# Heads in pairs on the row halves of the scores, and the next graph's products spread between this graph's stages

## The chip, the core and the metric

The program runs on one NeuronCore of a Trainium2 chip. The number that counts is the device time of one launch, in microseconds (us), lower being better. Five things work side by side: TensorE (PE, matmuls, with PEld for its weight loads), VectorE (DVE), ScalarE (ACT), GpSimd (POOL), and SyncE (SP), which only issues DMAs. They meet through semaphores. Every engine carries out its own instructions in the order in which they are written.

## What is computed

Sixteen graphs of 512 nodes with 384 features go through two attention layers, each with a layer norm, a ReLU and a residual. The first has 6 heads of 64 features with a softmax over masked scores; the second has 12 heads of 32 features, whose scores come from a sum of one source and one destination value, a leaky ReLU and a masked softmax, then an ELU and a gate.

```python
h = relu(layernorm(x))
q, k, v = heads(h @ Wq + bq), heads(h @ Wk + bk), heads(h @ Wv + bv)
probs = softmax(q @ k.T / sqrt(64) + where(adj, 0, -9e15))          # 6 heads
x = x + (probs @ v) @ Wf + bf
h = relu(layernorm(x))
f = h @ W                                                          # 12 heads of 32
a = leaky_relu(tanh(f) @ w_src + (tanh(f) @ w_dst).T)
o = elu(softmax(where(adj, a, -999)) @ f + b)
g = sigmoid(h @ H_w.T + H_b)
x = x + g * o + (1 - g) * h
```

## The kernel before

Everything of a graph stays on the chip. 512 nodes are four tiles (TT) of 128 partitions, 384 features three chunks (FC). A product in `fp32r` is made of three terms, high times high, high times low and low times high, so every operand has a `_hi` and a `_lo` tensor; `three` issues the nine matmuls of such a product. ACT makes the high part out of PSUM (`turned_high`, `qk_hi`, `ctx_high`), DVE the low part (`turned_low`, `qk_low`, `ctx_low`).

The order is written out by hand: each engine has a function `graph(b, more)` that is one turn of a loop over the graphs, and semaphores tie the five orders together. In one turn PE does, in this order:

- **first attention**: `turn_probs(b, h, c)` transposes a chunk of a head's probabilities into a `turn` bank (line 1094), DVE (even c) or ACT (odd c) copies it to `pT`, and `context` multiplies it with `v_tok` (line 1113). Between the turns of head h stand the `scores` of head h + 2 (lines 1083 and 1084), the products for q and k of the third pair of heads, and the transposes of half the mask.
- **projection and second norm**: `by_node(b, "out", ...)`, residual, statistics, `turn_norm`, one gate product.
- **features and logits**: `by_feature(..., "w1", c)`, `logits`; then DVE, ACT and PE in turns make the rows from which the second layer's weights come (`uq`, `r_rows`), beside `turn_feat` and the gate products.
- **aggregation**: `spread` puts four heads' rows into four banks (line 1154); in 12 steps DVE makes three edge tiles (line 818), ACT and POOL the fourth (lines 581, 584 and 412), and `aggregate` adds eight matmuls on quarters of the array's columns (lines 1170 and 1174). After the steps 0 to 7 PE also does the next graph's `turn_norm`, four of its q and k products and a `values` product; before step 11 stand its first two scores.
- **tail**: `turn_sums` (line 1187) with the next graph's scores and the rest of `values` between; DVE's `divide`, `positive`, `difference`, ACT's `elu` and POOL's `add_out` finish this graph, and SP stores it.

A score tile is one head by 128 queries by 512 keys. The head's 64 features fill only half the rows, so q's high and low part lie under each other in `qs`, k's high part is there twice in `kh` (POOL copies it, `double_keys`), and `kl` holds k's low part with zeros below: two full 128-row matmuls give three terms. DVE adds the mask and takes the minimum (`maxima`, line 771) into the two-deep ring `sm`, ACT takes the exponential (`exps`, line 533), DVE the reciprocal of the sum (`inverse`, line 776, once per head), POOL multiplies (`normalise`, line 356).

Eight PSUM banks: two `work`, two `score`, two `turn`, two `acc`. The work banks are handed out in alternation by the place of a product in the list TURN. The turned input `hT_hi`/`hT_lo` exists once, so the next graph's `norm1` may only be turned in after this graph's last gate product.

```python
q = qs[:, s, i, t * P:(t + 1) * P]
nc.tensor.matmul(score[n % 2][:], q, kh[:, s, i], start=True, stop=False)
nc.tensor.matmul(score[n % 2][:], q, kl[:, s, i], start=False, stop=True).then_inc(score_full, 1)
```

## Time and profile before

| what | value |
|---|---|
| device time, three runs | 2077.71, 2081.09, 2085.63 us, median 2081.09 |
| the profiled execution's span, first to last instruction | 2077.5 us |
| PE busy | 1859.4 us, 90% |
| DVE busy | 1414.8 us, 68% |
| ACT busy | 1201.8 us, 58% |
| POOL busy | 1098.2 us, 53% |
| DMA | 46.29 MB, mean 22 GB/s |

No separate time outside the span is given for the profiled execution; the median is 3.6 us above its span. PE's busy time counts a matmul from its start to its modelled end, and neighbours overlap by some 0.16 us, so the pace of a stream of matmuls is read from start to start in the timeline.

### The profile page before, as it was taken

The numbers are of one execution on the slowest core, as the hardware profiler recorded it, in microseconds if no ns is written. First come the engines' busy times: TensorE is split into PE (matmuls) and PEld (weight loads), VectorE is DVE, ScalarE is ACT, GpSimd is POOL, SyncE is SP. The second block draws the span as 40 slices with busy tenths as digits, with TensorE's granted clock in tenths as the row PEclk, the third lists the DMA queues.
The fourth block names the chain that finished last, engine by engine and source line by source line (L and its number), as shares of the span: only waits on it lengthen the run. The fifth ranks groups of instructions, "written<-read, shape, count | busy, mean of one in ns | idle before, by whom it ended". The sixth has DMA issues, their size and how long they took to land.

```text
span 2077.5 us, 35937 instructions
## 1 busy us (share of the span) xinstructions
PE 1859.4 (90%) x10608; PEld 1117.5 (54%) x10608; DVE 1414.8 (68%) x3115; ACT 1201.8 (58%) x2311; POOL 1098.2 (53%) x1383
## 2 busy tenths in 40 slices
PE   5998898988999989899999999889898899999986
PEld 4555555555554555546556465555555555455552
DVE  5667576675757667586775857757667575766757
ACT  4566465664656656565564656646566465665654
POOL 3455555464554655445554555555546455465545
PEclk9999999999999999999999999999999999999999
DMA  4001001010000101001010010100101000010000
GB/s 135 1 1 51 0 11 39 0 50 0 20 31 0 50 0 50 0 0 50 0 50 0 4 47 0 50 0 11 39 0 50 0 21 30 0 50 0 31 1 16
DMA packets 38101, 46.29 MB, mean 22 GB/s; under 512 B 2624, under 2 KB 38080, under 8 KB 38080
## 3 DMA queue, kind: packets, MB, share of 16 engines
q1 hardware_dynamic: 38080, 46.03, 6.7%
q8 instruction: 11, 0.18, 0.0%
q14 instruction: 10, 0.08, 0.0%
HBM read 33.44 MB, written 12.58 MB: 22 GB/s over the span
## 4 chain that ended last, share of the span: by engine, by line
PE 42%; issue 21%; POOL 19%; DVE 9%; ACT 7%; DVEq 0%; POOLq 0%; ACTq 0%
PE work L1022 16%; PE acc L1170 7%; PE acc L1174 6%; POOL arena L356 6%; POOL fin_g L421 4%; ACT arena L533 3%; POOL xres L435 3%; PE turn L1094 3%; PE acc L1133 2%; PE score L1083 2%; POOL xres L423 2%; POOL arena L403 2%; POOL arena L412 2%; DVE arena L818 2%; PE score L1084 2%
## 5 line engine op out<-in xcount | busy, mean ns | idle before, releaser
L533 ACT ACTIVATE arena<-sm,nmax 128x512 f32<-128x512 f32 x384 | 275.9, 719 | 142.3 <-DVE nmax L771 140.7
L412 POOL TENSOR_TENSOR arena<-arena,adjT 128x512 f32<-128x512 f32 x192 | 224.0, 1167 | 249.2 <-ACT arena L584 242.4
L356 POOL TENSOR_SCALAR arena<-arena,rinv 128x512 f32<-128x512 f32 x384 | 281.7, 753 | 126.6 <-DVE rinv L776 126.6
L771 DVE CUSTOM_DVE_ANT_0 sm<-score,mask 128x512 f32<-128x512 f32 x384 | 255.0, 680 | 66.3 <-PE score L1084 50.9
L818 DVE SCALAR_TENSOR_TENSOR arena<-score,uqT,adjT 128x512 f32<-128x512 f32 x384 | 269.8, 744 | 16.7 <-PE acc L1174 11.4
L1094 PEld LDWEIGHTS turn<-ident_f,arena 128*128 128x128 f32 x1536 | 180.6, 140 | 137.5 <-issue 78.3
L1094 PE MATMUL turn<-ident_f,arena 128*128 128x128 f32 x1536 | 242.8, 278 | 12.6 <-POOL arena L356 7.7
L1170 PE MATMUL acc<-arena 128*32 128x512 f32 x1536 | 204.5, 604 | 38.7 <-POOL arena L412 28.0
L786 DVE COPY arena<-turn 128x512 f32<-128x512 f32 x192 | 132.4, 689 | 129.2 <-PE turn L1094 128.4
L1083 PE MATMUL score<-kh,qs 128*128 128x512 f32 x384 | 183.6, 478 | 39.3 <-DVE nmax L771 39.2
L1174 PE MATMUL acc<-arena,u_den 128*32 128x512 f32 x1536 | 200.2, 592 | 0.0
L1113 PE MATMUL acc<-arena,v_tok 128*64 128x512 f32 x768 | 193.0, 609 | 5.6 <-DVE arena L786 5.6
L545 ACT ACTIVATE arena<-turn 128x512 f32<-128x512 f32 x192 | 112.8, 587 | 129.9 <-PE turn L1094 127.8
L364 POOL TENSOR_TENSOR rstd<-var,mhalf 128x1 f32<-128x1 f32 x128 | 68.3, 551 | 216.4 <-DVE var L730 216.4
L581 ACT ACTIVATE arena<-turn,nqT 128x512 f32<-128x512 f32 x192 | 131.1, 683 | 66.8 <-PE turn L1154 63.5
L1084 PE MATMUL score<-kl,qs 128*128 128x512 f32 x384 | 151.9, 396 | 0.0
L584 ACT ACTIVATE arena<-arena,uqT 128x512 f32<-128x512 f32 x192 | 138.8, 723 | 6.3
L818 DVE SCALAR_TENSOR_TENSOR arena<-turn,uqT,adjT 128x512 f32<-128x512 f32 x192 | 142.4, 742 | 0.0
L403 POOL TENSOR_TENSOR arena<-arena,uqT 128x384 f32<-128x384 f32 x64 | 60.3, 942 | 147.3 <-DVE uqT L936 147.3
L421 POOL TENSOR_TENSOR fin_g<-arena 128x384 f32<-128x384 f32 x64 | 73.2, 1144 | 120.2 <-DVE arena L848 115.5
L743 DVE SCALAR_TENSOR_TENSOR hT_lo<-work,hT_hi 128x384 fp32r<-128x384 f32 x128 | 70.8, 554 | 81.6 <-ACT hT_hi L501 81.4
L496 ACT ACTIVATE hn<-xres,shift,rstd 128x384 f32<-128x384 f32 x64 | 45.3, 707 | 137.9 <-DVE shift L735 137.9
(138 smaller groups left out, 4100.5 us busy)
## 6 DMA issues: line engine op xcount, KB each, us to landing
x_in<-in_x SPq DMA_DIRECT2D x16, 768.0 KB, 5.8
xres<-in_x SPq DMA_DIRECT2D x16, 768.0 KB, 4.6
out_x<-xres SPq DMA_DIRECT2D x64, 192.0 KB, 1.9
adj_u<-in_adj SPq DMA_DIRECT2D x16, 256.0 KB, 6.0
arena<-in_wq SPq DMA_DIRECT2D x1, 576.0 KB, 6.3
arena<-in_wk SPq DMA_DIRECT2D x1, 576.0 KB, 7.4
arena<-in_wv SPq DMA_DIRECT2D x1, 576.0 KB, 8.5
arena<-in_wf SPq DMA_DIRECT2D x1, 576.0 KB, 9.6
```

The lines of the kernel that those rows point to most:

```text
L356: nc.gpsimd.tensor_scalar(pr, pr, rinv[:, h, t:t + 1], 1.0, ALU.mult, ALU.mult).then_inc(probs_ready, 1)
L412: nc.gpsimd.tensor_tensor(edge[:, (n * HG + HG - 1) % 8], t_ring[:, n % 2], adjT[:, n % TT], ALU.mult).then_inc(last_edge_ready, 1)
L533: nc.scalar.activation(probs[h % 3][:, t], sm[:, i % 2], ACT.Exp, scale=-1.0, bias=nmax[:, h, t:t + 1], accum_out=rsum[:, h, t:t + 1]).the ...
L771: nc.vector.tensor_tensor_reduce(sm[:, i % 2], score[i % 2][:], mask[:, t], 1.0, 3.0e38, ALU.add, ALU.min, nmax[:, h, t:t + 1]).then_inc(s ...
L818: nc.vector.scalar_tensor_tensor(out=edge[:, (n * HG + j) % 8], in0=rbank[j][:], scalar=uqT[:, c, q:q + 1], in1=adjT[:, c], op0=ALU.max, o ...
L1022: ins = nc.tensor.matmul(ps, l(c), r(c), start=(c == 0 and i == 0), stop=(c == FC - 1 and i == 2))
L1083: nc.tensor.matmul(score[n % 2][:], q, kh[:, s, i], start=True, stop=False)
L1084: nc.tensor.matmul(score[n % 2][:], q, kl[:, s, i], start=False, stop=True).then_inc(score_full, 1)
L1094: ins = nc.tensor.transpose(turn[c % 2][:, t * P:(t + 1) * P], probs[h % 3][:, t, c * P:(c + 1) * P], ident_f[:])
L1113: ins = nc.tensor.matmul(acc[p % 2][i * DH0:(i + 1) * DH0], v_tok[:, c, f:f + DH0], (pT_late if p == 2 else pT_early)[i][:, c], start=(c = ...
L1170: nc.tensor.matmul(acc[0][j * DH1:(j + 1) * DH1], h_tok[:, c, f:f + DH1], edge[:, (n * HG + j) % 8], start=(c == 0), stop=(c == TT - 1), s ...
L1174: ins = nc.tensor.matmul(acc[1][j * DH1:(j + 1) * DH1], u_den[:, c, g, j], edge[:, (n * HG + j) % 8], start=(n == 0), stop=(n == STEPS - 1 ...
```

## The change

**Scores.** `qs`, `kh` and `kl` go. `qk_hi` and `qk_lo` hold q and k of all three pairs, head 2p in rows 0 to 63 and head 2p + 1 in rows 64 to 127. A step of `scores(g, p, t)` makes the tiles of both heads: three terms by two heads, six matmuls of 64 rows, alternating between the row halves, each half into its own bank. `double_keys` and the zeros go; the copies of a product out of PSUM (`qk_hi_copy`, `qk_low`) are one instruction of 128 rows where there were two of 64. `ctx_hi` and `ctx_lo` lie where q was.

**Order.** The six shared banks (two `work`, four `score`) are given out by a table, HOME, with two semaphores each; `turn` banks are now the work banks. Attention goes by pairs p: for each chunk c both heads are turned, then come score tiles of pair p + 1, then the context of chunk c - 1; `inverse` and `normalise` go tile by tile. `sm` is four deep. There are two turned-input buffers, `hT[0]` for the first norm and `hT[1]` for the second, so the next graph's norm1, its statistics and its q, k products move out of the aggregation: norm1's statistics stand between pairs 0 and 1 on DVE (and `root`, `norm1` on POOL), its turns in pair 2, k0 behind attention, k1 and k2 in the second norm, q0 before `uq`, q1 before the last gate product, q2 at the end. `gate` product 0 now stands before `logits(2)`, all four adjacency turns behind `out`.

```diff
-            def scores(g, h, tiles=range(TT)):
-                s, i = (h // 2) % 2, h % 2
...
-                    q = qs[:, s, i, t * P:(t + 1) * P]
-                    nc.tensor.matmul(score[n % 2][:], q, kh[:, s, i], start=True, stop=False)
-                    nc.tensor.matmul(score[n % 2][:], q, kl[:, s, i], start=False, stop=True).then_inc(score_full, 1)
+            def scores(g, p, t):
...
+                for i in range(2):
+                    bank_free(pe, g, "s", p, t, i)
+                q = slice(t * P, (t + 1) * P)
+                terms = ((qk_hi, qk_hi), (qk_lo, qk_hi), (qk_hi, qk_lo))
+                for n, (l, r) in enumerate(terms):
+                    for i in range(2):
+                        rows = slice(i * DH0, (i + 1) * DH0)
+                        ins = nc.tensor.matmul(bank_of(g, "s", p, t, i)[:], l[rows, 0, p, q], r[rows, 1, p],
+                                               start=(n == 0), stop=(n == len(terms) - 1))
...
+HOME = {
+    ("k", 0): 0, ("k", 1): 5, ("k", 2): 2, ("q", 0): 1, ("q", 1): 1, ("q", 2): 0,
...
+    ("fin", 0): 1, ("fin", 1): 0, ("fin", 2): 0, ("fin", 3): 0,
+}
...
+S_TILES = ((0, 1), (2,), (3,), ())
...
             def graph(b, more):
+                for p in range(NPAIR):
+                    for c in range(TT):
+                        turn_probs(b, p, c)
+                        if p + 1 < NPAIR:
+                            for t in S_TILES[c]:
+                                scores(b, p + 1, t)
+                        elif more:
+                            turn_norm(b + 1, 0, c)
+                        if c > 0:
+                            context(b, p, c - 1)
+                    context(b, p, TT - 1)
```

PE in the aggregation:

```diff
                 for n in range(STEPS):
                     if more and n == STEPS - 1:
-                        scores(b + 1, 0, (0, 1))
+                        scores(b + 1, 0, 0)
                     aggregate(b, n)
...
-                    if n == 3:
-                        hT_ready(b + 1, "norm1")
-                    if n in (3, 4, 5, 6):
-                        query_key(b + 1, (n - 3) // 2, "kq"[n % 2])
-                    if n == 7:
-                        values(b + 1, 0)
```

DVE: the statistics behind the first pair, and the tail:

```diff
+                    if p == 0 and more:
+                        dve.wait_ge(x_loaded, 16 * b + 32)
+                        for step in (tile_stats, mean, variance, shifts):
+                            for t in range(TT):
+                                step(b + 1, 0, t)
...
+                for t in range(TT):
+                    inverse_den(b, t)
+                    if more and t < 2:
+                        maxima(b + 1, 0, t + 2)
+                    divide(b, t)
+                    if more:
+                        inverse(b + 1, 0, t)
+                    if t > 0:
+                        difference(b, t - 1)
+                    positive(b, t)
+                difference(b, TT - 1)
+                if more:
+                    qk_low(b + 1, 2, "q")
```

POOL in the tail:

```diff
-                add_out(b, 0)
-                if more:
-                    normalise(b + 1, 0)
-                add_out(b, 1)
-                add_out(b, 2)
-                add_out(b, 3)
+                for t in range(TT):
+                    if more:
+                        normalise(b + 1, 0, t)
+                    if t > 0:
+                        add_out(b, t - 1)
+                add_out(b, TT - 1)
```

PE, in attention: a turn is line 1094 before and 989 now (`arena` is where the probabilities lie), scores are lines 1083 and 1084 before and 978 now, context is line 1113 before and 1005 now. Before, one head:

```order
L1094 MATMUL turn<-ident_f,arena 128x128 x4
L1083 MATMUL score<-kh,qs 128x512
L1084 MATMUL score<-kl,qs 128x512
L1094 MATMUL turn<-ident_f,arena 128x128 x4
L1083 MATMUL score<-kh,qs 128x512
L1084 MATMUL score<-kl,qs 128x512
```

Now, a pair:

```order
L989 MATMUL work<-ident_f,arena 128x128 x8
L978 MATMUL score<-qk_hi 128x512 x2
L978 MATMUL score<-qk_hi,qk_lo 128x512 x2
L978 MATMUL score<-qk_lo,qk_hi 128x512 x2
L1005 MATMUL acc<-arena,v_tok 64x512 x2
L989 MATMUL work<-ident_f,arena 128x128 x8
```

Four score matmuls for a pair of tiles became six on half the rows, and every step now passes from whole-array turns to row halves to column halves and back.

DVE, between the first and the second pair: 667 to 681 are the statistics of the next graph's norm1 (672, 676 and 681 the last of them), 722 is the copy of a turned chunk, 712 `maxima`; REGISTER_ALU and ISA rows without operands prepare a wait. Now:

```order
L670 REGISTER_ALU
L672 BN_AGGR mv<-stats 128x2
L676 TENSOR_SCALAR var<-mv 128x1 x4
L681 SCALAR_TENSOR_TENSOR shift<-mv,rstd 128x1 x4
L722 COPY arena<-work 128x512
L275 REGISTER_ALU
L708 REGISTER_ALU
L712 ISA sm,nmax<-score,mask 128x512
```

Before, in the same place, between the second and the third head's turns:

```order
L771 ISA sm,nmax<-score,mask 128x512
L771 ISA nmax 128x1
L757 SCALAR_TENSOR_TENSOR kl<-work,bias_c,kh 64x512 x2
L776 RECIPROCAL rinv<-rsum 128x4
L791 SCALAR_TENSOR_TENSOR ctx_lo<-acc,bias_c,ctx_hi 128x512
L786 COPY arena<-turn 128x512
```

The statistics, whose last four instructions wait for POOL's `root`, came from behind the second norm to ahead of a copy for which PE's turn bank waits.

DVE, in the tail: 825 (759 now) reads a turned sum, 831 (764) is `divide`, which frees its work bank, 848 (777) `difference`, 842 (772) `positive`. Before:

```order
L825 RECIPROCAL rden<-work 128x12
L765 REGISTER_ALU
L771 ISA sm,nmax<-score,mask 128x512
L771 ISA nmax 128x1
L830 REGISTER_ALU
L831 TENSOR_TENSOR arena<-work,rden 128x384
L848 SCALAR_TENSOR_TENSOR arena<-arena 128x384
```

Now:

```order
L759 RECIPROCAL rden<-work 128x12
L708 REGISTER_ALU
L712 ISA sm,nmax<-score,mask 128x512
L712 ISA nmax 128x1
L708 REGISTER_ALU
L712 ISA sm,nmax<-score,mask 128x512
L712 ISA nmax 128x1
L764 TENSOR_TENSOR arena<-work,rden 128x384
L718 RECIPROCAL rinv<-rsum 128x2
L777 SCALAR_TENSOR_TENSOR arena<-arena 128x384
```

Two score tiles now stand between reading a turned sum and dividing it, and the divide frees the bank in which PE's next `values` product or turn is due.

## Rows read from the trace of the kernel before

**Rows 1.** First lines of the page: the span, and busy time by engine.

```profile
span 2077.5 us, 35937 instructions
...
PE 1859.4 (90%) x10608; PEld 1117.5 (54%) x10608; DVE 1414.8 (68%) x3115; ACT 1201.8 (58%) x2311; POOL 1098.2 (53%) x1383
```

**Rows 2.** Stretches: length, busy of PE, PEld, DVE, ACT, POOL, clock, DMA.

```profile
1013.36:1056.29 42.93, 40.72 (x276) 18.67 (x275) 34.63 (x54) 26.70 (x43) 23.43 (x28) 1.00 0.00 0
1056.29:1069.48 13.19, 10.66 (x59) 8.40 (x56) 11.27 (x28) 8.38 (x20) 8.31 (x8) 1.00 0.04 15
1069.48:1108.76 39.28, 36.67 (x203) 22.02 (x201) 24.09 (x57) 24.67 (x55) 23.00 (x31) 1.00 0.18 62
1108.76:1124.19 15.43, 12.91 (x67) 10.78 (x66) 10.23 (x28) 5.89 (x11) 7.09 (x11) 0.89 0.00 0
1124.19:1133.50 9.31, 9.30 (x33) 5.45 (x33) 2.50 (x15) 4.50 (x8) 5.59 (x10) 1.00 0.00 0
1133.50:1139.95 6.45, 5.72 (x34) 4.62 (x34) 4.98 (x13) 4.57 (x9) 0.80 (x1) 1.00 0.00 0
2027.90:2060.90 33.00, 27.39 (x214) 9.17 (x213) 25.63 (x38) 18.06 (x28) 18.42 (x20) 1.00 0.01 1
```

**Rows 3.** Timeline of PE in the last graph's aggregation: start, us, instruction, wait.

```profile
2027.90 0.62 PE L1154 MATMUL score<-r_rows,pick 128*128 128x512 f32 x2
...
2038.49 0.72 PE L1154 MATMUL score<-r_rows,pick 128*128 128x512 f32 x2
...
2042.50 1.07 PE L1170 MATMUL acc<-arena 128*32 128x512 f32 x8 [0.97 <-POOL arena L412]
...
2048.49 0.73 PE L1154 MATMUL score<-r_rows,pick 128*128 128x512 f32 x2
```

**Rows 4.** Timeline of PE in attention: turns, scores and context.

```profile
1087.37 0.61 PE L1094 MATMUL turn<-ident_f,arena 128*128 128x128 f32 x4
...
1088.29 0.60 PE L1094 MATMUL turn<-ident_f,arena 128*128 128x128 f32 x4
...
1097.48 0.66 PE L1094 MATMUL turn<-ident_f,arena 128*128 128x128 f32 x4
1098.07 1.08 PE L1113 MATMUL acc<-arena,v_tok 128*64 128x512 f32 x4
1099.08 0.66 PE L1094 MATMUL turn<-ident_f,arena 128*128 128x128 f32 x4
```

**Rows 5.** Timeline of PE: first and last of a product's nine matmuls, and the next.

```profile
1080.43 0.40 PE L1022 MATMUL work<-hT_hi,wk_hi 128*128 128x512 f32 x1
...
1082.54 0.40 PE L1123 MATMUL work<-ident_b,mask 128*128 128x128 bf16 x4
```

**Rows 6.** Groups of weight loads: busy us, mean ns, idle before.

```profile
L1094 PEld LDWEIGHTS turn<-ident_f,arena 128*128 128x128 f32 x1536 | 180.6, 140 | 137.5 <-issue 78.3 <-POOL arena L356 16.3 <-DVE arena L786 10.8
L1084 PEld LDWEIGHTS score<-kl,qs 128*128 128x128 f32 x384 | 73.4, 191 | 0.7
```

**Rows 7.** Timeline of DVE: norm1's statistics, from first to last.

```profile
997.05 1.93 DVE L721 BATCH_NORM_STATS2 stats<-x_in 128x6 f32<-128x384 f32 x4
...
1001.56 0.16 DVE L735 SCALAR_TENSOR_TENSOR shift<-mv,rstd 128x1 f32<-128x1 f32 x1 [0.36 <-POOL rstd L364]
```

**Rows 8.** Groups of the page: the chain from a turned chunk to probabilities.

```profile
L533 ACT ACTIVATE arena<-sm,nmax 128x512 f32<-128x512 f32 x384 | 275.9, 719 | 142.3 <-DVE nmax L771 140.7
...
L356 POOL TENSOR_SCALAR arena<-arena,rinv 128x512 f32<-128x512 f32 x384 | 281.7, 753 | 126.6 <-DVE rinv L776 126.6
L771 DVE CUSTOM_DVE_ANT_0 sm<-score,mask 128x512 f32<-128x512 f32 x384 | 255.0, 680 | 66.3 <-PE score L1084 50.9
...
L786 DVE COPY arena<-turn 128x512 f32<-128x512 f32 x192 | 132.4, 689 | 129.2 <-PE turn L1094 128.4
```

**Rows 9.** Timeline of POOL in the tail: two starts of `add_out`.

```profile
1070.00 1.01 POOL L421 TENSOR_TENSOR fin_g<-arena 128x384 f32<-128x384 f32 x1
...
1072.24 1.01 POOL L421 TENSOR_TENSOR fin_g<-arena 128x384 f32<-128x384 f32 x1
```

More of the change, by code:

```diff
@@ L63 @@
[L63 to L80 removed]
+NSM = 4
@@ new lines, with both, attention_order @@
+for _t in range(TT):
+    HOME["norm1", _t] = 2 + _t
+    for _p in range(NPAIR):
+        for _i in range(2):
+            HOME["turn", _p, _t, _i] = _i
+            HOME["s", _p, _t, _i] = 2 + 2 * (_t % 2) + _i
+S_TILES = ((0, 1), (2,), (3,), ())
+def both(name, p, t):
+    return [(name, p, t, 0), (name, p, t, 1)]
+def attention_order():
+    order = []
+    for p in range(NPAIR):
+        for c in range(TT):
+            order += both("turn", p, c)
+            if p + 1 < NPAIR:
+                for t in S_TILES[c]:
+                    order += both("s", p + 1, t)
+            else:
+                order += [("norm1", c)]
+    return order
@@ new lines, with of_next @@
+FIRST = ([("norm1", t) for t in range(TT)]
+         + [("k", 0), ("q", 0), ("k", 1), ("k", 2), ("q", 1), ("q", 2), ("v", 0), ("v", 1), ("v", 2), ("v", 3)]
+         + [x for t in range(TT) for x in both("s", 0, t)])
+TURN = attention_order() + MIDDLE + TAIL
+def of_next(name):
+    return name[0] in ("norm1", "k", "q", "v") or name[:2] == ("s", 0)
+LAST = [x for x in TURN if not of_next(x)]
+def place(g, *name):
+    bank = HOME[name]
+    first, turn, last = ([x for x in order if HOME[x] == bank] for order in (FIRST, TURN, LAST))
+    if of_next(name):
+        if isinstance(g, int) and g == 0:
+            return bank, first.index(name)
+        return bank, len(first) + (g - 1) * len(turn) + turn.index(name)
+    own = last if isinstance(g, int) and g == B - 1 else turn
+    return bank, len(first) + g * len(turn) + own.index(name)
@@ L474, in _ @@
             make_mask(0)
-            double_keys(0, 0, (mask_ready, 1))
-            double_keys(0, 1)
-            normalise(0, 0)
+            for t in range(TT):
+                normalise(0, 0, t)
             with pool.Fori(0, B - 1) as b:
@@ L760, in qk_low @@
-                mark_drained(ins, g, name, p)
-            def maxima(g, h, tiles=range(TT)):
-                for t in tiles:
-                    i = h * TT + t
-                    dve.wait_ge(score_full, g * NH0 * TT + i + 1)
-                    if i >= 2:
-                        dve.wait_ge(exp_ready, g * NH0 * TT + i - 1)
-                    settle(dve)
-                    nc.vector.tensor_tensor_reduce(sm[:, i % 2], score[i % 2][:], mask[:, t], 1.0, 3.0e38,
-                                                   ALU.add, ALU.min, nmax[:, h, t:t + 1]).then_inc(smax_ready, 1)
@@ L929, in graph @@
                 gate_sum(b, 1)
+                if more:
+                    qk_low(b + 1, 0, "q")
                 filled(dve, b, "uq", 0)
@@ new lines, in graph @@
+                    context(b, p, TT - 1)
+                if more:
+                    hT_ready(b + 1, 0)
+                    query_key(b + 1, 0, "k")
+                pe.wait_ge(split, len(names))
+                pe.wait_ge(ctx_ready, (b + 1) * NPAIR)
+                for t in range(TT):
+                    by_node(b, "out", ctx_hi, ctx_lo, "wf", t)
+                for c in range(TT):
+                    turn_adj(b, c)
+                turn_norm(b, 1, 0)
+                turn_norm(b, 1, 1)
@@ L1309, in _ @@
                 values(0, t)
-            scores(0, 0)
-            scores(0, 1)
+            for t in range(TT):
+                scores(0, 0, t)
             pe.wait_ge(consts_ready, 1)
```

840 lines of the change are left out of this document (375 added, 465 removed).

## The prediction, made before the changed kernel was run

> **What bounds the kernel now.** I read the page's first lines, then the stretches of one graph in the middle, then PE's timeline inside each, then what each gap waits for. PE is busy 90% of a span of 2077.5 us, the next engine, DVE, 68% [rows 1]. The stretches cut one turn of 126.6 us at PE's landmarks [rows 2]: aggregation 42.9 (first spread to last aggregate), tail 13.2, attention 39.3, projection with the second norm 15.4, features and logits 9.3, and 6.45 to the next spread. PE is busy 40.7 of the 42.9, 36.7 of the 39.3, 9.3 of the 9.3, but 10.7 of 13.2 in the tail and 12.9 of 15.4 in the second norm, where the clock also falls (mean 0.89). So PE's order bounds it nearly everywhere, with some 10 us of gaps a graph. A change pays only by fewer PE columns, or by putting PE work into those gaps without opening others.
>
> How large can others be? The last graph shows it: its aggregation has none of the next graph's work, and takes 33.0 us with PE busy for 27.4 [rows 2]. There DVE's edges, and the ACT and POOL chain for the fourth edge tile, set the pace: the spreads are 10.6 and 10.0 us apart, and the aggregate waits 0.97 us for POOL [rows 3]. So 12 us of PE work stood in this stage before and cost 9.9. Taken out, it gives back 9.9 and must find room elsewhere.
>
> **Scores.** A turn of four transposes with one head's score tile takes 0.92 us [rows 4], and nine 512-column matmuls 2.11, 0.234 each [rows 5]. A pair of tiles was four such matmuls, 0.94 us. Now it is three terms of two. If the row halves run side by side as the column quarters do (eight aggregate records in 1.07 us, where the same number, at context's pace of four records in 1.01 by pairs, would take some 3.7 alone [rows 3, 4]), the pair costs 3 x 0.234 = 0.70; if one after the other, 1.40. No row shows two row halves at once, so these are both ends. I take 0.70, since column halves, the nearest form, overlap: two halves by two records make 1.01 us in context [rows 4]. The weights needn't stand in the way: a term needs two loads of 128 columns, which last 191 ns each, but loads of 140 ns follow each other every 0.11 us in the turns, so they overlap [rows 4, 6]. Changing the shape costs: a turn behind context takes 0.59 where behind scores it takes some 0.40 [rows 4]. I put 0.1 us on each side of a score step (between 0 and 0.2). So 0.9 against 0.94, twelve times a graph: nearly nothing, -0.5 us. POOL's doubling and the second halves of the copies go; in attention these engines were not the bound.
>
> The Trainium skill speaks here too. TensorEngine Tiling (Array Packing), section Tiling Modes, says that changing the tiling mode drains TensorE, which the trace agrees with for columns. TensorE: Matmul & The Clock Gate, Part 3, gives 3.07x for four row tiles, not 4x; an estimate from that page is 0.30 us a term instead of 0.234, 2.5 us a graph, and the sum would come to some 2120. No row here shows row tiles.
>
> **Aggregation, from 42.9 to 35.4.** Base is the last graph's 33.0. Added: q1 (2.1 us) ahead of gate 3, so DVE's gate_sum and qk_low come between edges(0) and edges(1), and edges(1) starts 2 us later; POOL's chain is late there too, so I count 0.65. The mask (four POOL operations, 2.75 us, between the fourth edges of steps 4 and 5) was covered by PE's products; now POOL is on the path: +1.4. The pair of scores before step 11 and its switches: +0.4 net of the gap there. Sum 35.4; bounds 33.9 (nothing but the scores) and 38.
>
> **Tail, from 13.2 to 18.5.** PE's work is now three pairs of scores, four values products of 1.6, four turns of sums of 0.4, and q2: 12.7 us. It hands banks back and forth with DVE. values(1) needs the bank of fin 0, whose divide stands behind two maxima of the score step between: gap 1.5. fin 2 needs fin 1 divided, behind the next two maxima (0.68 each [rows 8]), which only start when the scores after values(1) are full: gap 2.0. q2 ends at 16.8 and its bank is the first that the next attention turns into; ACT's and DVE's copies take until 18.4. POOL is as late: four normalise pairs of 1.35 with two add_outs of 2.24 between [rows 9] end near 18.6. Bounds: 14 (POOL and DVE keep up) and 21.
>
> **Attention, from 39.3 to 39.1 with k0.** For pairs 0 and 1 PE's steps sum to 11.1 us (32 turns 3.5, four score steps 3.6, four contexts 4.0). Behind the last turn stands a chain: copy 0.69, two maxima 0.68 each, two exponentials 0.72, inverse, normalise 0.75 [rows 8], about 5 us with hand-overs, beside two contexts of 1.0. So the next pair starts 12.4 us after this one, 1.3 of it idle. In pair 1 DVE first has the statistics, 4.7 us from first to last [rows 7], of which the four BN_STATS are 1.93 and the end waits for POOL's roots. Before they stood in the features stage, where DVE was idle (2.5 busy of 9.3 [rows 2]) and cost nothing. Now the copy of the first chunk is queued behind them, PE's second turn waits for its bank, and I get 2.4 us of gap and 15.0 for the pair. Pair 2 with norm1's turns: 9.5; k0: 2.2, which hides ctx 2's copies. Bounds: 36 (the chain is hidden), 42.
>
> **Second norm, from 15.4 to 13.8; features, from 9.3 to 11.3; to the spread, from 6.45 to 8.3.** Projection 6.4, adjacency 1.0, turns and k1, k2 fill what was idle, with 0.6 us of gaps: 13.8, now with 4.2 us of products in it. Gate 0 moved into the features: +1.7 with its switch. Before the spread stand q0 and its copies: qk_low is queued ahead of uqT on DVE, so `rlo` comes 1.9 us later.
>
> **The sum.** 35.4 + 18.5 + 39.1 + 13.8 + 11.3 + 8.3 = 126.4 against 126.6: -0.2 a turn, -3 us in fifteen. The first graph has two more products ahead of attention (+2), the last graph has no statistics and no fills (-5). My walk is at full clock; the stretch of before has one at mean 0.89, 15.4 x 0.11 = 1.7 us slower at most. Such falls follow weak PE stretches, and the new tail is one, so I add 0.5 us a graph: +7.5. Span 2077.5 - 3 - 3 + 7.5 = 2079; the median of the runs lies 3.6 above the span, so **2082 us**. Each graph's bound is off by perhaps 2 us either way, 30 in all: that is the true width.
>
> **Rivals.**
> (a) The row halves don't overlap fully, a slower outcome. Fully serial costs 0.70 x 12 = 8.4 us a graph, 126 in all: 2208. Half-way, with two weight loads of 0.19 as the pace (0.38 a term [rows 6]), 5 us a graph: 2158. The change pays nothing from 0.25 us a term on. For it: no row shows it done; against: the column tiles.
> (b) The new waits are smaller than I walk them, faster: the aggregation comes to 34, the tail to 16.5, pair 1 to 14: -4.4 a graph, 2016. For it: by my walk PE stands idle for about 6 us in the tail and 5 in attention, where before it was idle for 2.5 and 2.6 [rows 2], so hand-overs that overlap better than I count give much back.
> (c) The waits are larger: POOL is later in the tail (its two add_outs and four normalise pairs have no slack there), and the second norm's chain slips behind ACT's adjacency copies: +3 us a graph, 2127.
> (d) The products moved don't leave a mark at all and everything is as before: 2082, the same as the forecast.
>
> **Chances.** Forecast and (d), within 2065 to 2100: 0.32 (of it 0.05 faster, 0.21 same, 0.06 slower). (a) 0.2, (b) 0.33, (c) 0.15. A measurement of this kernel tells about 0.5% from no change, 10 us. Faster by more: 0.05 + 0.32 = 0.37; same: 0.21 + 0.02 = 0.23; slower: 0.40. The range for 8 in 10 takes in (b) to 2015 and (a) to its middle: 2015 to 2145.
>
> **What the new profile would show.** Score groups: six matmuls of 64 rows in about 0.7 us from first to last start, both halves starting within some 10 ns; (a) if they start 0.2 apart. The spreads 11 us apart, and the whole aggregation near 35. In attention a wait of PE for DVE's copy behind the statistics, 2 to 3 us once a graph, and POOL as releaser of the first turn of each pair. In the tail two gaps of 1.5 to 2 us behind DVE's divide. PE busy nearer to 85% than to 90%. If a graph takes 122 us, my waits in tail and attention were too long; if 130 or more, look at the score steps first.

## The result, and the profile of the changed kernel

The changed kernel takes 2182.34 us (median of four runs, 2181.36 to 2185.67), the kernel before 2082.4 in the same comparison: a ratio of 1.0496, 95% interval 1.0477 to 1.0516. The forecast was 2082, the range 2015 to 2145. The change makes the kernel 5% slower, and the prediction missed that.

The first lines of the page of after answer to [rows 1]; `PEclk` is from its view in 40 slices.

```profile
span 2183.5 us, 35601 instructions
...
PE 1870.5 (86%) x10992; PEld 1116.4 (51%) x10992; DVE 1369.7 (63%) x3114; ACT 1115.0 (51%) x2215; POOL 1039.1 (48%) x1287
...
PEclk9999999999999999999999999998999989989998
```

PE is busy 11 us more than before in a span 106 us longer, every other engine less. The time went into waits of PE, and part of PE's busy time is the lower clock: its mean is 0.963, where before it was 0.989.

One turn, for a graph in the middle (aggregation, tail, attention with k0, second norm, features, to the next spread). The columns are those of [rows 2]. Two landmarks lie 0.5 us earlier than there: the aggregation ends here with the start of its last matmul, the features with the start of the last logits product.

```profile
1061.06:1096.41 35.35, 30.00 (x228) 11.01 (x228) 27.31 (x42) 19.10 (x30) 21.14 (x24) 1.00 0.02 7
1096.41:1116.81 20.40, 14.73 (x87) 10.98 (x80) 14.98 (x36) 10.67 (x26) 10.00 (x10) 1.00 0.03 10
1116.81:1160.43 43.62, 39.13 (x213) 22.03 (x214) 26.01 (x75) 22.34 (x51) 24.75 (x35) 0.92 0.13 42
1160.43:1174.55 14.12, 13.13 (x83) 11.56 (x82) 10.19 (x26) 7.46 (x14) 7.25 (x11) 1.00 0.06 22
1174.55:1185.37 10.82, 10.82 (x42) 6.82 (x41) 1.10 (x2) 4.22 (x7) 0.77 (x2) 1.00 0.00 0
1185.37:1194.14 8.77, 7.89 (x45) 6.32 (x44) 5.94 (x16) 5.57 (x11) 0.68 (x1) 1.00 0.00 0
```

Graphs differ, so the comparison needs the mean of each stage over the first fourteen turns, cut at these landmarks, before and after. "Walked" is the prediction's own figure. By the landmark of [rows 2], to which the walked 35.4 and 18.5 belong, the two entries 35.35 and 20.4 of the last column are 35.9 and 19.9:

| stage | before | walked | after | after, at full clock |
|---|---|---|---|---|
| aggregation | 42.4 | 35.4 | 36.4 | 35.35 |
| tail | 13.7 | 18.5 | 21.1 | 20.4 |
| attention, k0 | 39.3 | 39.1 | 42.7 | 41.55 |
| second norm | 15.3 | 13.8 | 13.75 | 13.75 |
| features, to the spread | 16.3 | 19.6 | 19.6 | 19.6 |
| sum | 127.0 | 126.4 | 133.6 | 130.7 |

The last column is the length in graphs where the granted clock stayed at 2.4 GHz in that stage (the second norm varies between 13.4 and 14.1 at full clock, so its mean stands). Attention has three such graphs: 41.56 and 41.54 us where the tail before it was at full clock too, and 40.94 where the tail had a mean clock of 0.92; the first two stand in the table. Two rows to compare with the stretches above, an aggregation with a mean clock of 0.95 and an attention with 1.00:

```profile
926.44:963.40 36.96, 31.62 (x227) 11.41 (x228) 27.30 (x42) 19.08 (x30) 21.13 (x24) 0.95 0.02 7
...
322.55:364.11 41.56, 36.38 (x214) 20.62 (x214) 25.81 (x75) 22.02 (x51) 24.76 (x35) 1.00 0.14 44
```

So an aggregation takes 36.96 or 35.35 us, an attention 43.62 or 41.56, and the difference goes with the clock. Over the whole span the trace of after has 41 stretches at 1.2 GHz, 164 us together; before has 12, 50 us.

Which waits of PE there are, the view of waits shows, first of before and then of after (us in total, times, longest):

```profile
PE score L1083 <- DVE nmax L771: 39.2, 64, 0.9
PE acc L1170 <- POOL arena L412: 28.0, 34, 1.0
PE work L1037 <- ACT hn L496: 26.0, 45, 1.1
```

```profile
PE acc L1060 <- POOL arena L408: 68.0, 64, 2.1
PE work L989 <- POOL arena L374: 50.1, 76, 1.8
PE work L1076 <- DVE arena L764: 34.4, 17, 2.1
PE work L989 <- DVE qk_lo L697: 26.7, 14, 2.5
PE work L921 <- DVE arena L764: 22.9, 15, 1.5
PE work L989 <- DVE arena L722: 21.0, 15, 1.8
```

Before, the three longest sums were waits of at most 1.1 us, and after the first graph's start none was over 1.3. Now aggregates wait for POOL's fourth edge (line 408), the turns (line 989) for POOL's `normalise` (374), DVE's copy of q2 (697) and its copy of a chunk (722), and the tail's products and turns for DVE's `divide` (764). Each is over 20 us in all.

### The profile page after: what moved, and what is told of

Its sections match the earlier page's. It is cut to its first block, busy times and chain, and to the rows that moved or that the text cites. A ratio compares the mean times of both kernels' runs of the same rounds, so it can differ in the third digit from the quotient of the medians.

```text
span 2183.5 us, 35601 instructions
## 1 busy us (share of the span) xinstructions
PE 1870.5 (86%) x10992; PEld 1116.4 (51%) x10992; DVE 1369.7 (63%) x3114; ACT 1115.0 (51%) x2215; POOL 1039.1 (48%) x1287
## 4 chain that ended last, share of the span: by engine, by line
PE 49%; issue 20%; POOL 14%; DVE 10%; ACT 7%; POOLq 1%; DVEq 1%; ACTq 0%; DMA 0%
PE score L921 10%; PE work L921 8%; PE work L989 7%; PE score L978 6%; PE acc L1005 5%; POOL arena L408 4%; PE acc L1060 4%; PE acc L1064 4%; POOL arena L374 3%; DVE sm L712 3%; ACT arena L511 2%; PE acc L1024 2%; POOL arena L401 2%; POOL mask L366 1%; PE score L936 1%
## 5 line engine op out<-in xcount | busy, mean ns | idle before, releaser
L753 DVE SCALAR_TENSOR_TENSOR arena<-score,uqT,adjT 128x512 f32<-128x512 f32 x576 | 395.4, 744 | 104.8 <-PE acc L1064 93.1
L989 PE MATMUL work<-ident_f,arena 128*128 128x128 f32 x1536 | 248.3, 295 | 98.4 <-POOL arena L374 50.1
L989 PEld LDWEIGHTS work<-ident_f,arena 128*128 128x128 f32 x1536 | 178.2, 146 | 254.5 <-issue 127.9
L548 ACT ACTIVATE arena<-score,nqT 128x512 f32<-128x512 f32 x192 | 130.5, 680 | 213.8 <-PE score L1045 188.8
L517 ACT ACTIVATE arena<-work 128x512 f32<-128x512 f32 x192 | 114.0, 594 | 196.5 <-PE work L989 193.9
L722 DVE COPY arena<-work 128x512 f32<-128x512 f32 x192 | 132.0, 687 | 106.7 <-PE work L989 106.2
L1064 PEld LDWEIGHTS acc<-arena,u_den 128*32 128x32 f32 x1536 | 53.7, 113 | 119.7 <-issue 119.7
L978 PE MATMUL score<-qk_hi 64*128 64x512 f32 x384 | 98.8, 504 | 12.0 <-DVE nmax L712 11.0
L697 DVE SCALAR_TENSOR_TENSOR qk_lo<-work,bias_c,qk_hi 128x512 fp32r<-128x512 f32 x64 | 47.9, 749 | 86.3 <-ACT qk_hi L494 86.3
L921 PE MATMUL work<-wv_hi,hT_hi 128*128 128x384 f32 x192 | 75.1, 391 | 27.3 <-DVE arena L764 22.9
```

Of the source, the lines that this page charges most:

```text
L753: nc.vector.scalar_tensor_tensor(out=edge[:, (n * HG + j) % 8], in0=score[j][:], scalar=uqT[:, c, q:q + 1], in1=adjT[:, c], op0=ALU.max, o ...
L921: ins = nc.tensor.matmul(ps, l(c), r(c), start=(c == 0 and i == 0), stop=(c == FC - 1 and i == 2))
L978: ins = nc.tensor.matmul(bank_of(g, "s", p, t, i)[:], l[rows, 0, p, q], r[rows, 1, p], start=(n == 0), stop=(n == len(terms) - 1))
L989: ins = nc.tensor.transpose(bank_of(b, "turn", p, c, i)[:, t * P:(t + 1) * P], probs[p % 2 * 2 + i][:, t, c * P:(c + 1) * P], ident_f[:])
L1064: ins = nc.tensor.matmul(acc[1][j * DH1:(j + 1) * DH1], u_den[:, c, g, j], edge[:, (n * HG + j) % 8], start=(n == 0), stop=(n == STEPS - 1 ...
```

## Experiments

**First question: waits, clock or row halves?** In PE's timeline of attention in after, two score records (both halves of a term) start together, a term 0.23 us after the last, and a score step takes 0.90 us from its start to that of the context:

```profile
1122.50 0.50 PE L978 MATMUL score<-qk_hi 64*128 64x512 f32 x2
1122.84 0.39 PE L978 MATMUL score<-qk_hi,qk_lo 64*128 64x512 f32 x2
1123.07 0.40 PE L978 MATMUL score<-qk_lo,qk_hi 64*128 64x512 f32 x2
1123.40 1.08 PE L1005 MATMUL acc<-arena,v_tok 128*64 128x512 f32 x4
```

That was the forecast's number, so the row halves were no suspect. My theory was one part lower clock, one part waits in the tail and at pair 1. The next kernels took these one by one.

**e1_warm** fills PE's known waits with 34 products a graph that nobody reads.

```diff
+            def warm(k, n):
+                for _ in range(n):
+                    nc.tensor.matmul(acc[k][:, 0:D], w_hi["wk"][:, 0, 0:P], w_hi["wk"][:, 0, :], start=True, stop=True)
...
                 if more:
+                    warm(0, 6)
                     values(b + 1, 1)
                     scores(b + 1, 0, 3)
+                    warm(0, 8)
```

> The changed kernel with idle-filling matmuls on TensorE: 34 extra matmuls of 384 columns a graph (0.177 us each, 6 us a graph) into an accumulator bank that is overwritten afterwards, put just ahead of the waits of the tail, of the pair boundaries and of the copy behind the statistics. Theory C (the half clock, which the new waits bring on, costs about half of the 105 us lost): the time at half clock falls from 164 us to under 70 us and the kernel gets 20 to 50 us faster in spite of the added work, 2130 to 2165 us. Theory W (the waits alone are the cost, the half clock falls in places that wait anyway): unchanged or slower by up to 6 us a graph, 2180 to 2270 us.

2155.33 us, ratio 1.0334 (1.0314 to 1.0355), clock 0.987, time at 1.2 GHz 58 us in place of 164. PE is busy 53 us more, and the kernel is some 30 us faster. So the lower clock does cost time: about a third of the loss went with it, by the ratios. Every tail and every attention between the first graph and the last is at full clock in e1, and they take 20.4 and 41.56 us, as in after at full clock, so the fills lie inside the waits and lengthen no stage. What is left at 1.2 GHz stands mostly in the aggregation, behind the wait that follows the mask. The rest of the loss is waits and longer steps.

**e2_divide_first** puts `divide` ahead of the two maxima in the tail.

```diff
                     inverse_den(b, t)
+                    divide(b, t)
                     if more and t < 2:
                         maxima(b + 1, 0, t + 2)
-                    divide(b, t)
```

> The changed kernel with one swap on VectorE in the tail: divide stands ahead of the two maxima instead of behind them. Theory W: the gaps of 1.5 and 2.1 us before values(1) and the third turned sum shrink by 1.3 us each, the tail of 20.4 us gets 1 to 2.5 us shorter, 2145 to 2170 us. Rival P (GpSimd's chain of normalise and add_out ends the tail, the gaps on TensorE are slack): the gaps go and the time stays, 2178 to 2190 us.

2140.34 us, ratio 1.0263 (1.0241 to 1.0284), a little more than expected. The tail goes from 20.4 to 17.9 us in its median.

**e3_late_shifts** takes norm1's four `shifts`, which wait for POOL's roots, out from in front of pair 1's first copy.

```diff
                         elif more:
                             turned_low(b + 1, 0, c)
+                        if p == 1 and c == 0 and more:
+                            for t in range(TT):
+                                shifts(b + 1, 0, t)
...
-                        for step in (tile_stats, mean, variance, shifts):
+                        for step in (tile_stats, mean, variance):
```

> The changed kernel with the four shift instructions of norm1's statistics, which wait for GpSimd, moved behind the first copy and the first maxima of the second pair. Theory W: the wait of TensorE's second turn falls from 1.4 us by about 1.4 us, and with it 1 to 3 us a graph, 2135 to 2168 us. Theory C adds that a clock fall goes with it in some graphs. If the boundary chain hides it: 2178 to 2190 us.

2140.04 us, ratio 1.0266 (1.0246 to 1.0287); attention 42.7 to 40.55 in the mean. The wait it removes is seen in after, on DVE and then on PE:

```profile
1133.98 0.16 DVE L681 SCALAR_TENSOR_TENSOR shift<-mv,rstd 128x1 f32<-128x1 f32 x1 [0.48 <-POOL rstd L381]
...
1135.54 0.18 DVE L681 SCALAR_TENSOR_TENSOR shift<-mv,rstd 128x1 f32<-128x1 f32 x1 [0.36 <-POOL rstd L381]
1135.64 0.68 DVE L722 COPY arena<-work 128x512 f32<-128x512 f32 x1
```

```profile
1136.37 1.09 PE L989 MATMUL work<-ident_f,arena 128*128 128x128 f32 x8 [1.38 <-DVE arena L722]
```

**e4_halves_in_turn** writes head 0's three terms and then head 1's three, to price the overlap.

```diff
-                for n, (l, r) in enumerate(terms):
-                    for i in range(2):
+                for i in range(2):
+                    for n, (l, r) in enumerate(terms):
```

> The changed kernel with the six score matmuls of a pair of tiles in another order: all three terms of the first head, then all three of the second, so that the row halves can't run side by side for two of three terms. If side by side is worth 0.234 us a term, this costs 0.47 to 0.7 us per pair of tiles, twelve a graph: 60 to 130 us more, 2240 to 2315 us. If the score steps are hidden behind other waits: under 40 us more. If the halves gain nothing by alternating: unchanged.

2185.55 us, ratio 1.0503 (1.0469 to 1.0537): no change, so the expectation of 60 to 130 us more fell. The records say why: the first terms of both heads start 10 ns apart though two other matmuls stand between them in the order as written, and the step is as long as before:

```profile
431.17 0.51 PE L978 MATMUL score<-qk_hi 64*128 64x512 f32 x2
431.51 0.40 PE L978 MATMUL score<-qk_hi,qk_lo 64*128 64x512 f32 x2
431.74 0.40 PE L978 MATMUL score<-qk_lo,qk_hi 64*128 64x512 f32 x2
432.07 0.64 PE L1060 MATMUL acc<-arena 128*32 128x512 f32 x4
```

**e11_halves_serial** forces the order with a wait.

```diff
-                for n, (l, r) in enumerate(terms):
-                    for i in range(2):
+                for i in range(2):
+                    if i == 1:
+                        filled(pe, g, "s", p, t, 0)
+                    for n, (l, r) in enumerate(terms):
```

> The changed kernel with the six score matmuls of a step in the order head 0's three terms, head 1's three, and a wait of PE between for the first three to be done. It asks what the overlap of the row halves is worth. A score pair then takes 1.4 us plus one wait of PE for its own semaphore (0.1 to 0.3) in place of 0.70. If PE is the bound at all score steps: 12 x 0.9 = 11 us a graph, 160 us more than the changed kernel, 2345. If PE's time at the score steps in the tail and at the pair boundaries lies beside other engines' work: half of that or less, 2230 to 2260. If the halves did not overlap in the first place, nothing changes but the wait, 12 x 0.2 = 2.4 us a graph, 2220.

2429.93 us, ratio 1.170 (1.166 to 1.174). In its timeline one head's three terms take as long as both heads' did, then comes the wait, then the other head:

```profile
1244.63 0.50 PE L980 MATMUL score<-qk_hi 64*128 64x512 f32 x1
1244.97 0.39 PE L980 MATMUL score<-qk_hi,qk_lo 64*128 64x512 f32 x1
1245.21 0.39 PE L980 MATMUL score<-qk_lo,qk_hi 64*128 64x512 f32 x1
1245.65 0.49 PE L980 MATMUL score<-qk_hi 64*128 64x512 f32 x1
```

A step is 1.02 us to the other head's first term, and some 0.9 more for that head, 1.9 in place of 0.90: 1.0 more, 12 us a graph, if all of it counted. At full clock the stages show 7.5 of these: aggregation 36.35 for 35.35, tail 22.2 for 20.4, attention 45.6 for the 40.94 that stands, like it, behind a tail below full clock. The measured loss is 248 us, more than I expected in any case: 447 us of this span are at 1.2 GHz (clock 0.908), 283 more than in after. So the overlap is real, and rival (a) is refuted. What it is worth by itself isn't measured apart: of the 1.0 us a step 0.70 are the second head's three terms, and 0.3 the forced wait.

**Second question: do the waits add up, and which others are there?**

**e5_both** is e2 and e3 together.

> Divide ahead of the two maxima (as in e2_divide_first) and norm1's shifts behind pair 1's first chunk (as in e3_late_shifts), together. Theory S (the two waits stand in different stages and add up): 133.6 - 2.5 - 2.2 = 128.9 us a graph, about 2182 x (1.0263 + 1.0266 - 1.0496) = ratio 1.003 to before, 2090. Rival O (the gain of one is given back at the other's place, or the chip's clock takes it, since a quicker hand-over in one stage lets PE meet the next wait sooner): ratio 1.012 to 1.026, no better than the better of the two.

2105.43 us, ratio 1.0125 (1.0107 to 1.0144). Better than either, by 35 us, not by the 50 that the sum of ratios gives. The time at 1.2 GHz is 122 and 109 us in the single edits and 68 here, in the profiled run; that was the fastest of the four, and the mean clock of the other three (0.978 to 0.981) gives 80 to 93.

**e6_mask_spread** adds: the next graph's four mask operations one to a step on POOL, and not four in a row.

```diff
                     if more and n == 4:
                         filled(pool, b, "adj", TT - 1)
-                        make_mask(b + 1)
+                        pool.wait_ge(adj_loaded, 16 * (b + 1) + 16)
+                        settle(pool)
+                    if more and 4 <= n < 4 + TT:
+                        mask_part(n - 4)
```

> e5_both with the next graph's four mask operations on POOL one to a step behind the fourth edges of steps 4 to 7, instead of four in a row behind step 4. Theory M (POOL's 2.75 us in a row delay the fourth edge of step 5 and with it PE's aggregate): aggregation shorter by about 1.4 us a graph, 20 us in all under e5_both. Rival (the chain of the fourth edge is slack there, as DVE's three edges set the pace): same as e5_both within 5 us; or each single operation of 0.69 us delays its own step as much, which comes to the same total.

2078.31 us, ratio 0.999 (0.9976 to 1.0004): 27 us less. In e5_both, POOL's operations and PE's aggregate behind them:

```profile
1039.07 2.67 POOL L366 TENSOR_SCALAR mask<-adj_u 128x512 bf16<-128x512 uint8 x4
1041.82 2.28 POOL L408 TENSOR_TENSOR arena<-arena,adjT 128x512 f32<-128x512 f32 x2
```

```profile
1043.03 1.06 PE L1063 MATMUL acc<-arena 128*32 128x512 f32 x8 [2.06 <-POOL arena L408]
```

That wait goes and the aggregation is 33.87 us in every graph (35.35 at full clock before this edit). The difference, 1.48, is the price that the prediction gave the mask (1.4).

**e7_inverse_first** adds to e5_both: `inverse` of tile c - 1 ahead of the maxima of tile c.

```diff
-                            maxima(b, p + 1, c)
                             if c > 0:
                                 inverse(b, p + 1, c - 1)
+                            maxima(b, p + 1, c)
```

> e5_both with the inverse of tile c - 1 ahead of the maxima of tile c on DVE in attention. Theory P (at the turn to the next pair PE waits for POOL, which does several normalises in a row since their inverses came late): the first turn of pairs 1 and 2 comes about 0.7 us sooner each, 1.4 us a graph, 20 us in all. Rival D (the inverse waits for ACT's exponential, DVE stands there and maxima and the turn's copy come later, so PE waits for DVE's copy instead): 0 to 20 us slower than e5_both.

2109.97 us, ratio 1.0147 (1.0121 to 1.0174): no gain, if anything 4 us worse, the intervals overlap. PE's turns wait for `normalise` as long as before, 61 us in all against 56 in e5_both, so the last tile's is no sooner.

**e8_stats_early** adds to e5_both: norm1's statistics for the graph after next in the features stage; POOL's `root` and SP's load of x move with them and aren't shown.

```diff
                 if more:
                     qk_low(b + 1, 2, "k")
+                if more:
+                    dve.wait_ge(x_loaded, 16 * b + 48)
+                    for step in (tile_stats, mean, variance):
+                        for t in range(TT):
+                            step(b + 2, 0, t)
                 gate_sum(b, 0)
+                if more:
+                    for t in range(TT):
+                        shifts(b + 2, 0, t)
```

> e5_both with norm1's statistics for the graph after next moved out of attention altogether, into the features stage of this graph (x is loaded one graph further ahead; one more load of x at the end, not used). Theory V (what is left of the statistics' price in attention, four BN_STATS of 0.48 and the small steps ahead of the copy of pair 1's first chunk, is PE time): attention shorter by another 1 to 1.9 us a graph, 15 to 28 us under e5_both, and the features stage unchanged. Rival (in e5_both they already lie beside PE's work, or in the features stage they delay gate_sum and the logits' statistics on DVE, which PE waits for): same as e5_both within 5 us, or slower.

2106.15 us, ratio 1.0119 (1.01 to 1.0137): the same. With e3 this says that what cost time of the statistics was DVE standing and waiting for POOL's roots, and that the four BN_STATS lie beside PE's work.

**Third question: the hand-over from tail to attention.** In e6_mask_spread 14 of 17 stretches at 1.2 GHz begin 0.7 to 2.3 us after the first turn of a graph, and that turn has waited 1.64 us for q2's bank.

**e9_banks** is e6_mask_spread with three entries of the table changed.

```diff
-    ("k", 0): 0, ("k", 1): 5, ("k", 2): 2, ("q", 0): 1, ("q", 1): 1, ("q", 2): 0,
+    ("k", 0): 0, ("k", 1): 5, ("k", 2): 2, ("q", 0): 1, ("q", 1): 1, ("q", 2): 5,
...
-    ("fin", 0): 1, ("fin", 1): 0, ("fin", 2): 0, ("fin", 3): 0,
+    ("fin", 0): 1, ("fin", 1): 0, ("fin", 2): 3, ("fin", 3): 2,
```

> e6_mask_spread with three entries of the bank table changed: q2 from bank 0 to 5, the sums of tiles 2 and 3 (fin) from bank 0 to 3 and 2, so that they wait for maxima long done and not for DVE's divide of the tile before. Theory B (PE's waits in the tail for DVE's divide, 1.20 and 0.60 us, and at the first turn for q2's copy, 1.64, are waits for a bank): tail 17.9 to 16.1, and the first turn starts up to 1.6 us sooner, of which POOL's normalise of tile 3 takes back all but 0.5; together 2 us a graph, 30 us, to about 2050 (ratio 0.985). Rival N (POOL's last normalise bounds the first turn in any case, and it hangs on DVE's chain, not on the banks): the same as e6_mask_spread within 5 us.

2068.32 us, ratio 0.9947 (0.9929 to 0.9965): 10 us, not 30. The tail is 15.0 us in place of 17.9, more than I said, and attention 44.5 in place of 41.6: the wait has moved into the middle of the first turn, and has become one long one:

```profile
1182.50 0.70 PE L1000 MATMUL work<-ident_f,arena 128*128 128x128 f32 x3
1186.54 0.99 PE L1000 MATMUL work<-ident_f,arena 128*128 128x128 f32 x5 [3.34 <-POOL arena L379]
```

POOL's timeline has the cause: between the `normalise` pairs of tile 2 and of tile 3 (line 379) stand the two operations of `add_out(1)`:

```profile
1181.44 2.04 POOL L379 TENSOR_SCALAR arena<-arena,rinv 128x512 f32<-128x512 f32 x2
1183.46 1.29 POOL L421 TENSOR_TENSOR fin_g<-arena 128x384 f32<-128x384 f32 x1
1184.83 0.99 POOL L423 TENSOR_TENSOR xres<-fin_g,xres 128x384 f32<-128x384 f32 x1
1185.79 1.36 POOL L379 TENSOR_SCALAR arena<-arena,rinv 128x512 f32<-128x512 f32 x2
```

**e10_banks_pool** adds to e9_banks: it takes them out from between.

```diff
                 for t in range(TT):
                     if more:
                         normalise(b + 1, 0, t)
-                    if t > 0:
-                        add_out(b, t - 1)
-                add_out(b, TT - 1)
+                    if t == 1:
+                        add_out(b, 0)
+                for t in range(1, TT):
+                    add_out(b, t)
```

> e9_banks with POOL's four normalise pairs of the tail ahead of add_out(1), where add_out(1) (2.3 us) stood between those of tiles 2 and 3. Theory N2 (once the banks are free, POOL is what the first turn waits for): the first turn, all eight transposes of it, 1.5 us sooner than in e9_banks, 20 us in all, and the half-clock stretch behind it goes in most graphs (half-clock time 88 us in e6_mask_spread, under 50 here), another 10: about 2025 (ratio 0.973). Rival (the store of the tiles is later by as much and the next graph's residual load with it; or DVE's inverse of tile 3 is as late): same as e9_banks within 5 us.

2018.05 us, ratio 0.9701 (0.9678 to 0.9725): 50 us less than e9_banks, and 3% faster than the kernel before. The first turn waits 1.30 us in place of 3.34, and the time at 1.2 GHz falls from 81 to 44 us: of a graph's 3.4 us of gain 2.0 are the wait, the rest the clock. Its turn in the middle of the program, tail and attention:

```profile
1020.35:1035.37 15.02, 14.05 (x87) 11.14 (x80) 12.60 (x34) 9.37 (x25) 6.88 (x7) 1.00 0.00 0
1035.37:1076.30 40.93, 36.42 (x214) 20.58 (x213) 27.16 (x77) 23.00 (x53) 27.95 (x38) 1.00 0.15 50
```

**e12_first_turn** asks whether that was hidden behind the other waits: the changed kernel with q2 in bank 5 and this order on POOL, and nothing else.

> The changed kernel with two edits only, those that the first turn of attention waits for: q2 in bank 5 in place of 0, and POOL's normalise pairs of tiles 2 and 3 ahead of add_out(1). The question is whether the 50 us that this order on POOL gave in e10_banks_pool are there in the changed kernel itself, or only once the other waits are gone. Theory F (PE's 1.9 us wait at the first turn, and the half clock that follows it in nearly every graph, are one cause): the first turn 1 to 1.5 us sooner, its attention at full clock, together 2.5 to 3.4 us a graph: about 2135 (ratio 1.027). Rival D (the rest of the tail is late by DVE's divide behind the maxima, so tile 3's inverse comes too late for POOL to profit): under 10 us, 2172 or more.

2121.94 us, ratio 1.0196 (1.0172 to 1.022): 60 us less than after, more than theory F gave. So q2's bank and POOL's order together carry over half of the whole loss, and they do so without the other edits. But the gain isn't where theory F put it. The tail falls from 21.1 to 18.2 us in the mean, the aggregation from 36.4 to 35.4 (now at full clock in every graph), the second norm from 13.75 to 13.4. Attention stays as long, 43.0 for 42.7: in 13 of 15 graphs it has one stretch of 6.8 us at 1.2 GHz, which now begins 16.5 us after the first turn, behind the waits for POOL at the turn to pair 1:

```profile
1070.19:1088.41 18.22, 14.43 (x88) 11.19 (x81) 12.93 (x34) 9.90 (x25) 7.90 (x8) 1.00 0.03 11
...
1088.40:1131.50 43.10, 38.95 (x215) 22.02 (x214) 27.22 (x77) 22.98 (x53) 27.22 (x37) 0.92 0.14 43
```

## Why the prediction was wrong

**Right.** The score step: 0.90 us, said 0.9; the row halves overlap. The aggregation by the landmark of [rows 2]: 35.9 at full clock, said 35.4, with the mask at 1.48, said 1.4. Second norm 13.75, said 13.8. Features and the way to the spread 19.6, said 19.6. In the tail the two gaps behind `divide`, said 1.5 and 2.0, and the one for q2's bank, which the forecast's times (16.8 and 18.4) put at 1.6:

```profile
1103.14 0.45 PE L921 MATMUL work<-wv_hi,hT_hi 128*128 128x384 f32 x1 [1.53 <-DVE arena L764]
...
1107.98 0.55 PE L1076 MATMUL work<-ident_f,arena 128*128 128x128 f32 x3 [2.10 <-DVE arena L764]
...
1116.81 0.55 PE L989 MATMUL work<-ident_f,arena 128*128 128x128 f32 x3 [1.90 <-DVE qk_lo L697]
```

That the statistics cost through the shifts' wait for POOL was named, and e3 and e8 bear it out.

**Wrong, first step: the clock, "I add 0.5 us a graph".** The mean over the graphs is 2.9 us above the stages at full clock (133.6 against 130.7), where I allowed 0.5. I had taken the whole effect from one stretch of before, 1.7 us at most, and called the new tail one more of the kind. But I had myself walked six waits of 1.3 us and more into a turn in which before had none over 1.3. In the trace, stretches at 1.2 GHz stand behind such waits: in the tail behind those for `divide`, behind the first turn of attention, in pair 1 and the first steps of pair 2, and in the aggregation right behind the wait of 2.06 us for the fourth edge after the mask. So a wait can cost more than its length, by what PE does next: the aggregation with such a stretch is 1.6 us longer than without, pair 0 1.2 us (13.41 against 12.24), pair 1 0.9 us (16.75 against 15.85). Not every wait brings one: in after 9 of the first 14 aggregations have it. e1 shows the cause from one side (more work in the waits, less time at 1.2 GHz, less time in all), e11 agrees from the other.

**Wrong, second step: the tail's sum, "12.7 us" of PE work.** By the landmark of [rows 2], PE's stretch without its waits is 19.9 - 1.53 - 2.10 - 1.90 = 14.4 us. Four values products are 1.70 each and not 1.6, a turn of sums 0.53 and not 0.4, a score step 0.90, and q2 2.4: 6.8 + 2.1 + 2.7 + 2.4 = 14.0, with 0.4 in smaller hand-overs. The forecast gave no price for q2 or the score steps there, so which of the other terms of its 12.7 was short can't be read from it; its own times hold 0.6 of hand-overs, 13.3 in all. That is 1.1 us, and with waits longer by 0.4 the tail is 19.9 us where 18.5 was said, 1.4 a graph. The aggregation, 35.9 against 35.4, adds 0.5.

**Wrong, third step: the pairs of attention, "12.4", "15.0" and "9.5".** Pair 0, pair 1, and pair 2 with k0 in a graph whose tail and attention were at full clock:

```profile
322.55:334.79 12.24, 11.95 (x73) 6.50 (x73) 7.87 (x23) 7.60 (x19) 8.12 (x12) 1.00 0.34 112
334.79:350.64 15.85, 12.27 (x75) 6.66 (x73) 11.58 (x41) 8.70 (x22) 10.11 (x17) 1.00 0.00 0
350.64:364.11 13.47, 12.15 (x72) 7.46 (x70) 6.37 (x11) 5.72 (x12) 6.53 (x8) 1.00 0.12 34
```

That is -0.2, +0.85 and +1.8 against 12.4, 15.0 and 9.5 + 2.2, some 2.4 us a graph in all. The wait for POOL at the turn to the next pair is 1.3 us as said, but it falls inside the next pair's first turn, so pairs 1 and 2 have it and pair 0 hasn't. With it moved, 1.1 us is left over in pair 0, 0.85 in pair 1 and 0.5 in pair 2. In pair 0 part of it is the first turn of attention, which waits for POOL halfway through; behind the slower tail, where it doesn't, the pair took 11.62 us. For the rest the steps were summed short, as in the tail. In pair 1 two more waits of 1.38 and 0.60 stand, of the 2.4 said.

```profile
1149.04 1.00 PE L989 MATMUL work<-ident_f,arena 128*128 128x128 f32 x5 [1.00 <-POOL arena L374]
```

**The sum.** Second and third step: 4.3 us a graph (tail 1.4, aggregation 0.5, attention 2.4). The clock: 2.4 above the allowance. Fourteen turns: 94 us, less 6 since the mean of before is 127.0 and not the 126.6 of the graph that I cut. The first graph lost 9.5 us up to its first spread where I said 2: its attention starts 2.3 later and is 5.9 longer, with 13.7 us at 1.2 GHz in it where before had 3.4. The last turn and what follows it lost 4.9, where I said that they would win some 4.7. 88 + 7.5 + 9.6 = 105, which is the miss in the span (2183.5 against 2079).

**The rivals.** (a) fell with the first trace. (c), larger waits, was the case: +3 a graph and 2127, with POOL's two `add_out` named as the cause. That is where e12 found over half of the loss, but (c) had no term for the clock, which took 2.9 a graph. The range ended at 2145, since (c) was added to nothing. (b), with smaller waits, came to 2016. That e10 took 2018 is luck and not its confirmation: the order was changed for it, and its stages are others than those of (b), the tail 15.0 where (b) has 16.5, attention at full clock 40.9 where (b) has 38.1.

## What to carry to other kernels

When products are moved to fill gaps, walk the hand-overs of the helper engines too, and put what the next stage's first instruction waits for ahead of what only the end of this one needs: here two operations on POOL and one bank together cost 60 us of 2182. Give new waits a price for the clock as well: here it came to 2.9 us a graph, beside three waits of 1.5 to 2.1 us in the tail, three of 1.0 to 1.4 in attention and one of 2.1 in the aggregation. Look at which stretches are at the lower clock before and after each edit: they point at the wait to take next.

## What the runs showed of the hardware

- Matmuls on different row halves that write different banks run side by side even when written one half after the other (e4: 10 ns between the halves' first terms, no change in time). The Trainium skill, TensorE: Matmul & The Clock Gate, Part 3, has matmuls start strictly in the order in which they are written; the records of e4 don't agree for row halves, and the unchanged time speaks with the records. So the first section's sentence that every engine carries out its instructions in the order in which they are written doesn't hold for these matmuls either.
- A 64-row matmul of 512 columns takes as long as a pair on both halves (0.23 us from start to start in e11 and in after). The estimate from the figure for four row tiles in the same place of the Trainium skill, 0.30 us a term, does not hold for two halves here.
- A DVE operation beside one of POOL's can take over twice as long, and it depends on which: `positive` (line 772) took 0.55 us beside `normalise` (POOL line 374), as it did with POOL idle, and 1.35 beside the first operation of `add_out` (line 416), which ended 0.4 us before it. Over the whole trace the medians are 0.56 (41 of them) and 1.36 (20). So an `add_out` in the tail also delays the `divide` that is behind `positive` on DVE.

```profile
1108.37 0.55 DVE L772 SCALAR_TENSOR_TENSOR arena<-arena,hn 128x384 f32<-128x384 f32 x1
...
1110.39 1.35 DVE L772 SCALAR_TENSOR_TENSOR arena<-arena,hn 128x384 f32<-128x384 f32 x1
```

```profile
1110.03 1.30 POOL L416 TENSOR_TENSOR fin_g<-arena 128x384 f32<-128x384 f32 x1
```

What stays open: how much of the loss the clock alone makes. The fills of e1 gave some 30 us back, with 58 us still at 1.2 GHz. By the stages it is 2.9 us a turn in after and 0.5 in before, an estimate of some 36 us in fifteen turns; half of the 114 us more at 1.2 GHz, 57, is the most that it can be. The scores on row halves and the new order of the stages were changed together, and no run has one without the other, so how much the row halves by themselves give against the kernel before isn't shown.
